# Two cross-attention loops: the order of the maxima's turn, the latents' products and the next scores in odd steps

## The reference, cut to what matters

```python
ln = layer_norm(latents); xn = layer_norm(context)      # context: 16 x 1601 x 128
q = ln @ Wq                                             # 16 heads of 64
k, v = split(concat([xn, ln]) @ Wkv)                    # keys: 1601 context rows and 64 latents
w = softmax(mask(q k^T / 8))                            # the mask is in the second layer only
x = x + (w v) @ Wo
```

## Time and profile before

| | |
|---|---|
| time, median of 3 runs | 2043.71 us (2040.76 to 2045.15) |
| the profiled execution's own time | 2040.44 us |
| its span, first to last instruction | 2038.3 us |
| loop of x0, first product of step 0 to first product of step 15 | 77.3 to 795.9 us of the span |
| loop of x1, first product of step 16 to first product of step 31 | 1126.9 to 1840.2 us |
| busy over the span: PE, DVE, ACT, POOL | 94%, 80%, 63%, 45% |
| granted TensorE clock over the span | 0.975 of full speed |

### The profile page before, as it was taken

The page is one execution under the profiler, slowest core; times in us unless marked ns, Lnnn a source line. Parts: engine busy times, 40 slices in busy tenths (PEclk is TensorE's granted clock), DMA queues, the critical chain, the costliest instruction groups (busy, mean ns, idle before and its releaser), DMA issues. The chain is left out here.

```text
span 2038.3 us, 34984 instructions
## 1 busy us (share of the span) xinstructions
PE 1914.0 (94%) x12318; PEld 1026.9 (50%) x12318; DVE 1632.0 (80%) x3928; ACT 1279.2 (63%) x2295; POOL 912.2 (45%) x1000
## 2 busy tenths in 40 slices
PE   7899999999999999889788999999999999998886
PEld 6444545454454545533656445454545454544575
DVE  6789888888888887699676787878787878786657
ACT  4366666676767677444244787877777777777312
POOL 5586665666766662088231533333232323232004
PEclk9899999999999999989998999999999999999898
DMA  4322322222222120132104011111121111110100
GB/s 142 89 68 68 93 81 69 68 68 68 69 68 81 52 68 2 46 108 100 41 6 123 14 43 39 46 39 39 39 60 39 39 39 42 37 30 1 30 1 11
DMA packets 148854, 110.53 MB, mean 54 GB/s; under 512 B 120892, under 2 KB 136232, under 8 KB 148680
## 3 DMA queue, kind: packets, MB, share of 16 engines
q1 hardware_dynamic: 148680, 108.31, 19.1%
HBM read 65.15 MB, written 14.29 MB: 39 GB/s over the span
## 5 line engine op out<-in xcount | busy, mean ns | idle before, releaser
L1300 DVE TENSOR_TENSOR x_p_lo<-x_psum,x_p_hi 128x512 f16<-128x512 f32 (+1 forms) x864 | 581.0, 682 | 134.9 <-ACT x_psum L1058 134.8
L1057 ACT ACTIVATE x_p_hi<-x_psum 128x512 f16<-128x512 f32 (+1 forms) x448 | 268.8, 600 | 251.7 <-PE x_psum L903 195.9
L1057 ACT ACTIVATE x_p_hi<-x_psum,x_bcol 128x512 f16<-128x512 f32 (+1 forms) x416 | 289.8, 697 | 142.3 <-PE x_psum L903 133.5
L929 PE MATMUL x_psum<-x_p_hi,x_x_both 128*128 128x512 f16 (+1 forms) x832 | 317.3, 381 | 13.8 <-DVE x_p_lo L1300 10.7
L901 PE MATMUL x_psum<-x_q,x_xT_both 128*128 128x512 f16 x832 | 317.4, 381 | 4.3 <-DMA x_q<-x_shift_rows 4.3
L903 PE MATMUL x_psum<-x_q,x_xT_both 128*128 128x512 f16 x832 | 316.6, 381 | 0.0
L902 PE MATMUL x_psum<-x_q,x_xT_both 128*128 128x512 f16 x832 | 316.6, 380 | 0.0
L930 PE MATMUL x_psum<-x_p_lo,x_x_both 128*128 128x512 f16 (+1 forms) x832 | 315.9, 380 | 0.0
L931 PE MATMUL x_psum<-x_p_hi,x_x_both 128*128 128x512 f16 (+1 forms) x832 | 315.7, 379 | 0.0
L1245 DVE CUSTOM_DVE_ANT_0 x_junk<-x_psum,x_brow 128x512 bf16<-128x512 f32 (+2 forms) x512 | 279.1, 583 | 5.5 <-PE x_psum L980 3.4
L1248 DVE TENSOR_REDUCE x_mx<-x_psum 128x1 f32<-128x512 f32 (+2 forms) x512 | 276.2, 582 | 4.7 <-PE x_psum L980 4.7
(11 more groups left out here) (494 smaller groups left out, 3589.9 us busy)
## 6 DMA issues: line engine op xcount, KB each, us to landing
x_x_both<-context_rows SPq DMA_DIRECT2D x32, 832.0 KB, 5.1
context_rows<-x_x SPq DMA_DIRECT2D x16, 832.0 KB, 3.5
x_raw<-in_ctx SPq DMA_DIRECT2D x16, 768.0 KB
ssm_c_row<-ssm_bc_rows SPq DMA_DIRECT2D x16, 512.0 KB, 4.1
ssm_b_wide<-ssm_bc_rows SPq DMA_DIRECT2D x7, 512.0 KB, 3.5
x_mrow<-in_mask_BxS_bk SPq DMA_DIRECT2D x16, 200.1 KB
x_Wkv<-in_L_xattn_Wkv SPq DMA_DIRECT2D x4, 512.0 KB, 5.3
x_xT_both<-context_rows SPq DMA_TRANSPOSE x96, 3.9
```

The lines of the kernel that those rows point to most:

```text
L929: pe.matmul(out, v_hi, p_hi[r][rows, :], start=start, stop=False)
L1057: act.activation(p_hi[r][rows, :], score[r][rows, :], ACT.Exp, scale=SCORE_UNIT, **bias).then_inc(p_hi_ready, 1)
L1300: v.tensor_tensor(p_lo[r][rows, :], score[r][rows, :], p_hi[r][rows, :], ALU.subtract).then_inc(p_lo_ready, 1)
```

## The change

In odd steps PE now does the turn ahead of P(22) instead of behind it, and it does the latents' products ahead of S(0), S(1), S(2) of the next step instead of behind them. Even steps keep PE's order. The copy of an odd step's latents' products moves from ACT (two copies of 512 columns in unit 2 of the even step) to DVE (one copy of 1024 columns, ahead of `p_lo` of the even step's unit 0); the copy of an even step's stays on ACT. In x0 the guess of the root moves from unit 3 to unit 4 of odd steps, and the statistics beside it from units 3, 4, 5 to units 4, 5, 6.

```diff
-    GUESS_AT = 3
+    GUESS_AT = 4
...
+                def next_scores(u):
+                    if at.has_next and u > LAST - AHEAD + HOLD[at.par]:
+                        k = u + AHEAD - STEPS
+                        for k in range(0 if k == HOLD[at.par] else k, k + 1):
+                            scores(k, at.npar, at.half + STEPS, at.n, at.ni)
                 for u in range(STEPS):
                     if u + AHEAD < STEPS:
                         scores(u + AHEAD, at.par, at.half, at.b, at.i)
-                    elif at.has_next and u > LAST - AHEAD + HOLD[at.par]:
...
+                    elif at.par == 0:
+                        next_scores(u)
                     todo = [x for x in at.items.get(u, []) if x[0] != "lat"]
-                    if len(todo) > 1:
+                    if len(todo) > 1 or (at.par == 1 and todo == [("turn", 0)]):
                         aux_item(at, todo.pop(0))
...
                     products(u, at)
                     for item in todo:
                         aux_item(at, item)
+                    if u + AHEAD >= STEPS and at.par == 1:
+                        next_scores(u)
...
-                    if u == 2 and not (at.first and at.par == 0):
-                        latents_sums(at.half, 1 - at.par)
+                    if u == 2 and at.par == 1:
+                        latents_sums(at.half, 0)
...
-                    late = {3: [0], 4: [1, 2], 5: [3, 4]}
+                    late = {4: [0, 1], 5: [2, 3], 6: [4]}
...
+            def latents_sums(done):
+                v.wait_ge(pv_done, done)
+                v.tensor_copy(sum_l[:, :, 1, :], aux.rearrange("p (h l) -> p h l", l=L)).then_inc(aux_free, 2)
...
+                    if u == 0 and at.par == 0 and not at.first:
+                        latents_sums(at.half)
                     v.wait_ge(p32_ready, at.half + u + 1)
```

## The result

| | before | after |
|---|---|---|
| time, median | 2042.24 us (4 runs, 2040.53 to 2045.15) | **2023.06 us** (4 runs, 2020.42 to 2025.76) |
| ratio | | 0.9909, 95% interval 0.9893 to 0.9925 |
| the profiled execution | 2040.44 us | 2025.49 us |
| steps 1 to 14 and 17 to 30 together | 1342.2 us | 1324.3 us |
| even, odd step of x0 | 47.64, 48.37 us | 46.98, 47.44 us |

The change is faster by 0.9%: 19.2 us between the medians where 15.7 were forecast, 2023.1 us against 2028.0. A step counts here from its first product to that of the next step. The lengths in the table are those of nearly all steps of their kind (even: 2 to 12 and 20 to 30; odd: 3 to 11 and 19, 25, 27, 29).

A forecast was written before the change was run, and what follows sets the result against it. PE was taken to bound both loops, with waits hidden in its records. 14 x 0.99 - 0.3 (step 14) + 5 x 0.43 = 15.7 us, from a median of 2043.71 to 2028.0 us; range 2020 to 2037, eight in ten.

The forecast's parts named there:

- PE bounds the loops and loses by waits inside records: Both loops: PE sets the time; front of even steps hides 0.56 us (x0) and 0.76 us (x1) of waiting.
- rival 4: Whole kernel: no room, as busy time says; waits only move, 2041 to 2045 us; chance 0.06.
- rival 3: Even steps: gain given back inside because DVE cannot follow PE to the maxima; 2036 to 2041.5 us; chance 0.09.
- The turn: Odd steps, ahead of P(22): its 0.11 us on PE costs nothing, and DVE takes it 0.43 us earlier.
- 0.43 us of idling: Odd steps: DVE's wait for the turn, taken as the amount by which DVE's work behind it moves up.
- Rival 1: Turn brings nothing, DVE not ready earlier; only the start of even steps and the query part gain; 2034 us; chance 0.10.
- The latents' products ahead of S(0): End of odd steps: transfer hidden, P(0) 2.71 us behind S(0) in x0, 0.43 us earlier; x1 0.23 earlier.
- The front of even steps: P(0) to S(7): ACT relieved of a wait and two copies; all waiting gone, 0.56 us (x0), 0.76 (x1).
- The copy: On DVE before the even step's first `p_lo`: takes 1.20 us, hidden with 0.58 us to spare.
- Rivals 2 and 5: Copy takes 2.4 us: 2035 us, chance 0.06; DVE sets the pace of even steps, slower: 2058 us, chance 0.05.
- Guess and statistics: Odd steps of x0: query item 2 gains 0.90 us, item 3 waits 0.47; net 0.43 in steps 3 to 11.
- P(24): Odd steps: starts at 359.87 instead of 360.30 us, with 0.2 us of its wait for `p_lo` left.

The follow-up runs named there:

- e1_turn: Kernel before with one edit: in odd steps the turn stands ahead of P(22); 2036.24 us, ratio 0.9967.
- e4_copy_act: Changed kernel with the copy of odd steps' latents' products back on ACT, PE's order as changed; 2033.23 us, ratio 0.9950 to the kernel before.
- e5_copy_twice: Changed kernel with the DVE copy of odd steps' latents' products made twice in a row; 2031.17 us, ratio 0.9959 to the kernel before.
- g_first: Changed kernel with S(0) between P(25) and odd steps' latents' products, DVE's copy in two halves; 2021.45 us, ratio 0.9916 to the kernel before.

## Why the prediction was right, and where its sizes were off

- **PE bounds the loops and loses by waits inside records.** Right. Even steps gave back 0.66 and 0.87 us where busy time left 0.19 and 0.34; rival 4, no room, falls, and so does rival 3: nothing is given back inside the even steps, which gain more than the 0.57 and 0.77 us of their front.
- **The turn.** Free on PE, as said. Its size was low: 0.52 us, not 0.43. The step that failed is "0.43 us of idling": taken as all that can go, it leaves out the 0.09 us by which a DVE row that waits for nobody starts before the end of the one ahead. Rival 1, the turn brings nothing, falls with e1_turn.
- **The latents' products ahead of S(0).** Right: S(0) 0.75 behind them, P(0) 2.73 behind S(0) for 2.71 predicted. In x1, timeline of PE and of DVE at the start of step 26, beside the earlier trace rows:

```profile
1581.97 0.39 PE L901 MATMUL x_psum<-x_q,x_xT_both 128*128 128x512 f16 x1
...
1584.90 0.39 PE L929 MATMUL x_psum<-x_p_hi,x_x_both 128*128 128x512 f16 x1 [0.17 <-DVE x_p_lo L1312]
...
1590.20 0.38 PE L901 MATMUL x_psum<-x_q,x_xT_both 128*128 128x512 f16 x1
```

```profile
1584.15 0.69 DVE L1312 TENSOR_TENSOR x_p_lo<-x_psum,x_p_hi 128x512 f16<-128x512 f32 x1 [0.78 <-ACT x_psum L1064]
```

  2.93 us for 2.91. By its starts P(0) waits 0.125 us in x0 and 0.33 in x1, forecast 0.11 and 0.31. With the turn's 0.09, odd steps lost 0.94 and 0.28 us, forecast 0.86 and 0.23.
- **The front of even steps.** 5.30 us from P(0) to S(7) in both loops, forecast 5.31. Mis-sized was the claim that this is all: 0.09 (x0) and 0.10 us (x1) more goes behind S(7), in small waits at the maxima (in x1 0.01 us at a time) that I had not looked for. And both causes that I named count: with the order alone, about half of the gain is left (e4_copy_act).
- **The copy.** 1.23 us for 1.20, starts 0.93 after the latents' products for 0.95, hidden by 0.57 for 0.58. Rivals 2 and 5 fall, the latter by e5_copy_twice: 1.3 us more of DVE per even step cost 0.59 and 0.39, which is what stood out of the cover. The Trainium skill's rule (VectorE: DVE Perf Modes, section Specifications), ScalarE nearer to PSUM and VectorE to SBUF, agrees with the single operation (1.09 us for ACT's two copies, 1.23 for DVE's one), but moving the copy against it gained 4.7 us: where the operation stands in the queues counted for more than its own time.
- **Guess and statistics.** Right in each step. Timeline of PE and of DVE in step 7 of the changed kernel, beside the earlier trace rows:

```profile
413.56 0.38 PE L929 MATMUL x_psum<-x_p_hi,x_x_both 128*128 128x512 f16 x1
414.21 0.22 PE L960 MATMUL x_psum<-x_lnT_hi,x_qk_hi 128*128 128x128 f16 x1
...
417.31 0.23 PE L960 MATMUL x_psum<-x_lnT_hi,x_qk_hi 128*128 128x128 f16 x1 [0.30 <-DVE x_q L1238]
```

```profile
415.39 0.17 DVE L79 TENSOR_SCALAR x_xrt<-x_xrv 128x13 int32<-128x13 int32 x1
...
415.68 1.25 DVE L250 BATCH_NORM_STATS2 x_xstats<-x_raw 128x6 f32<-128x128 f32 x6
416.84 0.74 DVE L1238 SCALAR_TENSOR_TENSOR x_q<-x_psum,x_q 128x256 f16<-128x256 f32 x2
```

  Query item 2 follows P(2) by 0.65 us, without a wait; L79 no longer waits for POOL; item 3 starts 0.46 us late by its starts (a bracket of 0.30), forecast 0.47.
- **The sum.** 15.7 us were forecast for steps 1 to 14 and 17 to 30, 18.0 measured; the means of steps 3 to 14 and 19 to 30 are 47.16 and 47.34 us, forecast 47.3 and 47.4. The difference of 2.3 is the 0.05 to 0.09 at the turn and the 0.1 behind S(7), in 14 steps each. The median came out 4.9 us below the forecast: 2.3 are the steps, 1.5 are the median before, which is lower with its fourth run, and about 1 is scatter of the rest. Step 0 and the stage between the loops were 0.9 us shorter in this profile, but the stage lasted 330.6 and 332.3 us in two profiles of the changed kernel, so that part is not shown to be a gain.
- **Steps that depart from their kind.** Steps 17, 18, 21 and 23 of x1 gain up to 0.5 us more or less than their kind. For step 23 the trace of the kernel before shows why: S(0) of the next step stands 2.79 us behind the last shift row instead of 2.46, and in the changed order the latents' products cover that. Why for the others was not followed.
- **P(24).** Forecast was a wait of 0.2 us; its start is 0.11 late. It follows the start of its `p_lo` by 0.73 us (355.69 to 356.42), the same way as in the kernel before, so this is the forecast wait, less the 0.09 us that the turn gave beyond the forecast. The change from 128 to 65 rows has no part in it (g_first).

## What to carry to other kernels

On an engine whose records overlap, measure waits from start to start over a stretch with a known number of instructions; busy time hid two thirds or so of what even steps gained here. Ask of a copy or a statistic which queue idles at that moment, and what stands behind it there, before asking which engine does it faster: an item that waits for another engine at the head of an in-order queue holds what is ready behind it, and letting it come when its input is there paid three times (turn, guess, `out` item). When the time scatters by more than an edit is worth, compare the repeating steps, nearly all of which here agree to hundredths.

## What the runs showed of the hardware

- Ahead of and behind matmuls with 64 rows or 64 columns on the stationary side (the latents' products, S(26)) a matmul of 512 columns starts 0.31 us after the one ahead of it instead of 0.216: 128 to 64, 65 to 64 and 64 to 128 alike. Between 128 and 65 rows there is no such pause (0.216 us both ways, even steps). The Trainium skill (TensorEngine Tiling (Array Packing), section Tiling Modes) says that changing the tiling mode drains TensorE; both findings fit that, if 65 rows count as the mode of 128.
- The latents' products are six matmuls, in three pairs, one half of the columns each. The two of a pair run side by side: their record is 0.39 us together (357.82, x2), as long as that of one, so the six take 0.75 us of PE where three of 128 rows take 0.65.
- A DVE row that waits for nothing starts 0.07 to 0.09 us before the end of the row ahead; one wait costs that overlap besides its own length.
- The transfer of the shift rows lets S(0) start 2.45 to 2.48 us after the start of the DVE row ahead of it, in all kernels where it sets S(0); step 23 alone departs (2.71 to 2.96).
- The mean granted clock of one piece behind the second loop differs between executions that do the same work there (0.78 or 0.84), for 1.2 us. The whole of that part differs by up to 5 us between profiles; how much of this is the clock was not worked out.
